# A gated delta-rule attention layer with experts on one core: bias and identity products leave TensorE, the inverse is merged by VectorE, and the order of the four engines' work is another

## The reference

```python
x = x + layernorm(attn(layernorm(x)))
x = x + layernorm(ffn(layernorm(x)))

# attn: 8 key heads, 16 value heads of 128
mixed = silu(causal_conv4(h @ Wqkv.T + bqkv) + conv_b)      # q, k, v
z     = h @ Wz.T + bz                                       # 2048 gate values
beta  = sigmoid(h @ Wb.T + bb)
g     = -exp(A_log) * softplus(h @ Wa.T + ba + dt_bias)
q = q * rsqrt(sum(q*q) + 1e-6) * 128**-0.5
k = k * rsqrt(sum(k*k) + 1e-6)
def step(state, (q, k, v, g, b)):                           # over the tokens
    state = state * exp(g)
    delta = (v - k @ state) * b
    state = state + outer(k, delta)
    return state, q @ state
core = outs * rsqrt(mean(outs*outs) + 1e-6) * norm_w * silu(z)
attn = core @ Wout.T + bout

# ffn: one shared expert, and the top 8 of 16 small ones
```

## Time and profile before

| | |
|---|---|
| median of 3 runs | 3621.46 us (3620.43 to 3624.41) |
| the profiled execution, its own time | 3620.91 us |
| its span in the trace | 3619.1 us |
| busy share of the span | PE 91%, VectorE 75%, ScalarE 67%, GpSimd 60% |
| first load issued, first matmul starts | 7.8 us, 68.3 us |
| one chunk of the loop | 108.0 us, of which TensorE is busy 101.5 us |
| the loads of the start, all behind one semaphore | 13.2 MB, landed by 44.5 us |
| granted TensorE clock | 0.966 of full over the span |

### The profile page before, as it was taken

How to read it: one execution, slowest core, us unless ns; L and a number is a source line. 1 busy time by engine, 2 the same in 40 slices (tenths; PEclk the granted TensorE clock), 3 DMA queues, 4 the chain that set the end, 5 groups by cost and what they waited for, 6 DMA issues and landing times.

```text
span 3619.1 us, 86991 instructions
## 1 busy us (share of the span) xinstructions
PE 3296.9 (91%) x24003; PEld 2944.1 (81%) x24256; DVE 2712.9 (75%) x8608; ACT 2441.7 (67%) x5922; POOL 2162.0 (60%) x5380
## 2 busy tenths in 40 slices
PE   1799999999999999999999999999999999999986
PEld 1688888888888888888888888888888888888875
DVE  3577787777787877777877778777777877777763
ACT  1576777767777667677677676676676667676662
POOL 0676666666666666666666666666566666566660
PEclk9899999999999999999999999999999999999996
DMA  3111111111111111111111111111111111111110
GB/s 156 37 43 34 41 35 35 41 38 33 41 34 35 43 35 34 43 32 41 38 35 41 36 32 42 36 35 40 36 32 40 38 35 40 37 32 42 36 40 4
DMA packets 423099, 142.70 MB, mean 39 GB/s; under 512 B 211120, under 2 KB 421616, under 8 KB 422128
## 3 DMA queue, kind: packets, MB, share of 16 engines
q1 hardware_dynamic: 422768, 139.83, 14.9%
HBM read 93.11 MB, written 46.66 MB: 39 GB/s over the span
## 4 chain that ended last, share of the span: by engine, by line
PE 66%; DVE 10%; ACT 10%; issue 9%; DMA 1%; POOL 1%; SPq 1%; DVEq 0%; ACTq 0%; POOLq 0%
PE bF L450 9%; PE bB L617 6%; PE bQ L530 5%; PE bXT L538 5%; PE bS L587 4%; PE bS L595 3%; PE bB L674 3%; ACT L793 3%; PE bB L668 3%; PE bS L579 2%; PE bD L602 2%; PE bQ L469 2%; PE bX L543 2%; PE bXT L477 2%; PE bD L580 2%
## 5 line engine op out<-in xcount | busy, mean ns | idle before, releaser
L1101 DVE SCALAR_TENSOR_TENSOR Y<-bF,Cv,Y 128x127 f32<-128x127 f32 (+2 forms) x3072 | 851.3, 338 | 18.0 <-ACT Y L810 13.2
L881 ACT ACTIVATE XiT<-bXT 128x512 fp32r<-128x512 f32 x384 | 229.5, 598 | 534.0 <-PE bXT L538 534.0
L450 PE MATMUL bF<-XnT,Wqkv 128*128 128x128 f32 x4096 | 549.0, 284 | 0.0
L450 PEld LDWEIGHTS bF<-XnT,Wqkv 128*128 128x128 f32 x4096 | 521.2, 200 | 7.0 <-issue 1.7
L810 ACT ACTIVATE Y<-bF,Cv 128x128 f32<-128x128 f32 x1024 | 385.2, 461 | 83.5 <-PE bF L450 83.5
L1517 POOL TENSOR_TENSOR Tp<-Tp 32x64 f32<-32x64 f32 (+2 forms) x768 | 359.8, 468 | 60.2
L1144 DVE TENSOR_TENSOR Qi<-bQ,Cf 128x512 fp32r<-128x512 f32 x384 | 265.0, 690 | 127.3 <-PE bQ L530 126.9
L793 ACT ACT_TABLE_LOAD x257 | 329.7, 1283 | 5.3 <-PEq L1601 0.7
L1510 POOL TENSOR_TENSOR Tp<-Cb,Yb 32x64 f32<-32x64 f32 (+1 forms) x384 | 275.5, 717 | 32.7 <-POOL Yb L1519 4.9
L1510 POOL TENSOR_TENSOR Tp<-Yb,Tm 32x64 f32<-32x64 f32 (+1 forms) x384 | 274.7, 715 | 30.1
L1411 POOL TENSOR_TENSOR Ln<-Ex,KKQ 128x512 f32<-128x512 f32 x128 | 164.2, 1283 | 207.5 <-ACT Ex L872 132.1
(11 more groups left out here) (217 smaller groups left out, 9335.2 us busy)
## 6 DMA issues: line engine op xcount, KB each, us to landing
DL<-Ln SPq DMA_DIRECT2D x128, 256.0 KB, 2.3
XiT<-DX SPq DMA_DIRECT2D x128, 256.0 KB, 2.9
Xi<-DX SPq DMA_DIRECT2D x128, 256.0 KB, 3.3
DX<-Yb SPq DMA_DIRECT2D x256, 32.0 KB, 1.9
Xf<-x SPq DMA_DIRECT2D x32, 128.0 KB, 2.8
Wqkv<-wqkv SPq DMA_DIRECT2D x1, 4096.0 KB, 15.8
Cb<-DL SPq DMA_DIRECT2D x128, 32.0 KB, 1.9
Xr<-x SPq DMA_DIRECT2D x32, 128.0 KB, 2.9
```

The lines of the kernel that those rows point to most:

```text
L450: last = mm(bank[:, i, :], Wqkv[:, k, c:c + P], XnT[:, k, :], start=(k == 0), stop=(k == KT - 1))
L881: op(XiT[:, :, :], heads(bXT), ACT.Copy).then_inc(sem["xt_done"], 1)
L1101: last = stt(y, bank[:, i, 0:P - shift], Cv[:, g * TILES + tile, n:n + 1], y, ALU.mult, ALU.add)
```

## The change

Six edits come together.

1. **Loads.** Five small transfers get a semaphore of their own (`early`), are issued first, and alone hold up the setup. `Wqkv` comes in four pieces; `Wz`, the z bias and the rest have semaphores that their first readers wait for. `Wout` is scaled by VectorE ahead of its first use.
2. **Biases.** No bias products: VectorE adds the z bias (kept as f32 in `Zf`) out of PSUM into `Gz` (`gate_bias`), and ScalarE takes the SiLU of `Gz` in place; the bias of beta and a is added where VectorE copied them before.
3. **Sums of squares.** `ss` is gone. TensorE transposes all four of q and k (two before), and ScalarE squares the transposed tiles in four instructions that also sum along the row (`accum_out`). The squares now follow the transposes.
4. **No identity products.** `invert_begin` is gone. VectorE adds level 0 out of PSUM to the `XiT` and `Xi` that the DMA brought (`merged_t`, `merged`), and ScalarE copies for levels 1 and 2 only the new off-diagonal blocks.
5. **The last level** works on 64 rows and 64 columns.
6. **Another order** of the steps on every engine. `proj(a, 1, 1)` moves ahead of `az`, `D0` from the head of item 2 to the end of item 1, `ba` from the end of item 0 to the head of item 1, `ks_qs(w, 1)` behind level 0.

```diff
             def z_proj(f, part):
                 if part == 0:
                     pe.wait_ge(sem["convv_done"], at("convv_done", f))
-                    mm(bF1[:, :], onesb, Zb[:, c], start=True, stop=False)
-                    mm(bF1[:, :], XnT[:, 0, :], Wz[:, 0, c], start=False, stop=False)
+                    mm(bF1[:, :], XnT[:, 0, :], Wz[:, 0, c], start=True, stop=False)
-            def ss(f):
...
-                for i in range(2 * GK):
-                    last = mm(bXT[:, i:i + 1], Sq[:, i, :], ones[:, 0:1], start=True, stop=True)
             def ktr(f):
-                pe.wait_ge(sem["sse_done"], at("sse_done", f))
-                for kh in range(GK):
-                    last = nc.tensor.transpose(heads(bXT)[:, kh, :], QK[:, g, 2 * kh + 1, :], ident)
+                pe.wait_ge(sem["xt_done"], at("xt_done", ahead(f, -2)))
+                pe.wait_ge(sem["silu_done"], at("silu_done", f, 1))
+                for i in range(2 * GK):
+                    last = nc.tensor.transpose(heads(bXT)[:, i, :], QK[:, g, i, :], ident)
-            def invert_begin(v, front):
...
-                mm(bXT[:, :], IdR[:, 0, :], XiT[:, :, :], start=True, stop=True)
-                mm(bX[:, :], IdR[:, 0, :], Xi[:, :, :], start=True, stop=True)
+            def invert_q(v, n, front=None):
                 if n == 0:
+                    if front:
+                        pe.wait_ge(sem["ex_done"], at("ex_done", ahead(v, 1)))
...
+                    pe.wait_ge(sem["xb_in"], at("xb_in", v))
                     pe.wait_ge(sem["lnr_done"], at("lnr_done", v))
...
             def square_qk(f):
-                op(Sq[:, :, :], QK[:, f[1], :, :], ACT.Square).then_inc(sem["sq_done"], 1)
+                act.wait_ge(sem["ktr_full"], at("ktr_full", f))
+                for i in range(2 * GK):
+                    last = op(Sq[:, i, :], heads(bXT)[:, i, :], ACT.Square, accum_out=Ssq[:, i:i + 1])
             def gate(f):
-                op(Gz[:, f[1], :, :], heads(bF1), ACT.Silu).then_inc(sem["gz_done"], 1)
+                act.wait_ge(sem["zb_done"], at("zb_done", f))
+                op(Gz[:, f[1], :, :], Gz[:, f[1], :, :], ACT.Silu).then_inc(sem["gz_done"], 1)
+            def new_blocks(bank, buf, n, below):
+                b = BASE << n
+                for o in range(0, P, 2 * b):
+                    rows, cols = slice(o + b, o + 2 * b), slice(o, o + b)
+                    if not below:
+                        rows, cols = cols, rows
+                    last = op(buf[rows, :, cols], heads(bank)[rows, :, cols], ACT.Copy)
+                return last
+            def gate_bias(f):
...
+                tt(Gz[:, g, :, :].rearrange("p a b -> p (a b)"), bF1[:, :], Zf[:, g * GH * P:(g + 1) * GH * P], ALU.add)\
+                    .then_inc(sem["zb_done"], 1)
+            def merged_t(v):
+                dve.wait_ge(sem["xt_full"], at("xt_full", v, 1))
+                tt(XiT[:, :, :], heads(bXT), XiT[:, :, :].bitcast(F32), ALU.add).then_inc(sem["xt_done"], 1)
+            def merged(v):
+                dve.wait_ge(sem["x_full"], at("x_full", v, 1))
+                tt(Xi[:, :, :], heads(bX), Xi[:, :, :].bitcast(F32), ALU.add).then_inc(sem["xi_done"], 1)
+        EARLY = [(whole(d), src) for d, src in ((Xf, x[0]), (Cf, constf), (Cv, conv), (Wba, wba))]
+        EARLY += [(Gz[:, :, :, :].rearrange("p a b c -> p (a b c)")[:, 0:14 * P], consth)]
```

353 lines of the change are left out of this document (186 added, 167 removed).

## The result

The changed kernel takes 3700.53 us (median of 4 runs, 3694.61 to 3703.16) against 3620.94 (3618.95 to 3624.41) in the same job: ratio 1.0216, 95% interval 1.0199 to 1.0234. The prediction was 3600 with a range of 3500 to 3670, so it was wrong by 100 us, in sign and beyond its range. The profiled run has 3702.07 us and a span of 3700.3.

The account below looks back on a forecast made before the run. TensorE was taken as the bound, with little of its saved work felt because of the chain at each item's head. From 3620.9 us, −46 for the start and +24 for the loop gave 3599, said as 3600; range 3500 to 3670.

Parts of the forecast that it names:

- The start: Setup before the loop: early loads end sooner, first matmul near 22 us, 46 us earlier (lower bound 35).
- The squares: Head of an item on ScalarE: four squares out of PSUM take 1.1 us, upper bound 1.4.
- Merges and gate's bias at 0.68 us each: VectorE: two merges and the gate's bias, 0.68 us each; +1.8 us an item with a third saved.
- The head, 10.6 us to the first inversion product: Item 2, start to the inverse's first product through ScalarE's chain to `Ex`: 10.6 us, before 10.5.
- my 28.0 and 25.5: Forecast lengths in us of item 1 (before 25.8) and item 2 (before 25.9).
- VectorE becomes the bound: Rival, chance 0.25: merges and gate's bias felt in full in item 1, chunk +3.0 us, time 3665.
- The wait for `Ex` that I gave as a sign: Ahead of the inverse's first product: TensorE waits 1 us or more for ScalarE's `Ex` in every item.
- The sum by item, +0.8 us a chunk: Loop: four items sum to 108.8 us against 108.0, +0.8 us a chunk, +24 us in 30 chunks.
- VectorE's pause at the loop's turn stays as it is: Loop's turn: VectorE's pause unchanged, its list still ending with the result's two steps; slower clock behind it stays too.
- TensorE's work, 1.41 us an item less: TensorE per item: sums of squares and identity products go, z bias halves, two transposes come; 5.6 us a chunk less.
- the signs: What would show it right: among others, TensorE busy 88 to 90%, about 96 of a chunk's 109 us.
- my sum: Whole kernel: 3620.9 − 46 + 24 = 3599 us, given as 3600.

Follow-up runs that it names:

- before_start_products: Kernel before with the new start alone, both biases still TensorE products, the z bias split on 128x16: 3590.6 us, 0.9926 of before.
- changed_identity: Changed kernel with the first level's identity products and ScalarE's two full copies back in place of VectorE's merges: 3736.4 us, 1.0332 of before.
- changed_bias_product: Changed kernel with both biases as TensorE products again, 238 satisfied waits keeping TensorE's loop in its place: 3727.0 us, 1.0310 of before.
- order_fits: Changed kernel with bias and first-level identity products of before, Epq on ScalarE, waits ahead of all four lists against turn pauses: 3629.4 us, 1.0037 of before.
- start_fits_turn: start_and_turn with the small product Epq moved from VectorE to ScalarE, so VectorE's loop lies in three blocks: 3446.0 us, 0.9530 of before.
- turn_changed_60: Changed kernel with 60 more instructions (satisfied waits) ahead of TensorE's list, the loop itself the same: 3765.2 us, 1.0411 of before.
- start_and_turn: before_start_products with VectorE's list 23 and GpSimd's 20 instructions longer ahead of the loop: 3585.5 us, 0.9911 of before.
- changed_again: The changed kernel itself once more, unaltered, as reference for the runs beside it: 3692.8 us, 1.0220 of before.
- before_vector_fits: Kernel before with 21 more instructions (satisfied waits) ahead of VectorE's list: 3615.4 us, 0.9996 of before.

## Why the prediction was wrong, step by step

- *The start*: first matmul at 22.52 us, forecast 22, 45.8 us earlier. VectorE's chain begins at 17.07. Right. That the kernel would gain all of it was not: before_start_products gained 26 us.
- *The squares*: four in 1.00 us from start to start (1822.58 to 1823.58), forecast 1.1; 0.9 by the formula of the Trainium skill, "ScalarE: Activation LUTs". Between the two. The changed kernel's rows show what the formula leaves out, a second record each:

```profile
1822.58 0.30 ACT L843 ACTIVATE Sq<-bXT 128x128 f32<-128x128 f32 x1
1822.74 0.23 ACT L843 ACTIVATION_READ_ACCUMULATOR Sq<-bXT 128x1 f32 x1
1822.83 0.31 ACT L843 ACTIVATE Sq<-bXT 128x128 f32<-128x128 f32 x1
```

- *Merges and gate's bias at 0.68 us each*: 0.685, 0.679 and 0.690. Right. Taking them away gained nothing (changed_identity, changed_bias_product): the rival "VectorE becomes the bound" is refuted as a mechanism, though its time, 3665, was nearer. That was luck.
- *The head, 10.6 us to the first inversion product*: 11.09 in item 2 (1817.93 to 1829.02). `PartsT` began at 8.95, where I had it finished at 8.94; its 0.32 us and the hand-over make TensorE wait 0.66. That 0.5 us is as much as items 1 and 2 each have over my 28.0 and 25.5; that it is the same 0.5 us is not shown. The wait for `Ex` that I gave as a sign, 1 us or more in every item, is 0.43 us in three items of four; the chain is felt at three places instead, at Z, `PartsT` and `Ex`.

```profile
1826.88 0.32 ACT L875 ACTIVATE PartsT<-bXT 128x128 bf16<-128x128 bf16 x1
1827.55 0.38 PE L515 MATMUL bQ<-PartsT,Ch 128*128 128x128 bf16 x4 [0.66 <-ACT PartsT L875]
1829.02 0.63 PE L538 MATMUL bQ<-XiT,LnR 128*128 128x128 f32 x4 [0.43 <-ACT Ex L888]
```

- *The sum by item, +0.8 us a chunk*: this is the step that failed; the loop has +3.8. It took the order as nearly free. Where nothing pauses (order_fits against start_fits_turn), items 0 to 3 take 1.4, 2.6, 0.5 and 1.4 us more, with the bias and identity products still in. I had −1.1, +2.2, −0.4 and +0.1: the terms that were mis-sized are those of items 0 and 3 above all, where the head should have got shorter or stayed.
- *"VectorE's pause at the loop's turn stays as it is"*: its 2.7 us did stay. But I had nothing for pauses of TensorE's own, which came with the place of its shorter loop: 84 us in 29 turns, 2.9 a chunk. The first of them, 1.7 us, ends item 3, which has 29.6 us where I had 27.1; turn_changed_60, without it, has 27.7. So item 3 is over by 1.8 for the pause and 0.6 besides, items 1 and 2 by 0.5 each, and item 0 is under by 0.8 (27.4 for 28.2): 2.6 of the 2.7 us that the medians leave open. These 1.8 us are where the pause stands and not its price: turn_changed_60 took it away and got slower.
- *TensorE's work, 1.41 us an item less*: the signs had 96 us of a chunk busy, and it is 100. The sums of squares and the identity products went at about their price (3.4 and 2.2 us a chunk by start to next start). But groups that now stand ahead of a wait last longer: `new_state` 4.7 us a chunk instead of 3.6, `out_proj` 7.5 instead of 6.4. A cost read from start to next start in a full list leaves out the end of the last product, which a wait uncovers; that this is the reason is argued, not tested.
- *Whether the turn is to blame for the loss*: the pairs of runs do not say so. The turn costs the old order 4.8 us a chunk (start_and_turn against start_fits_turn). Against order_fits it costs the changed kernel 2.6 us (111.8 against 109.2). The bias and identity products are in order_fits and not in the changed kernel; changed_bias_product and changed_identity have 0.5 and 1.0 us a chunk more than changed_again, which gives 4.1 us for the turn as an estimate, and 4.3 of the 5.8 for the order. So the order with its head made the loop slower; the pauses changed places, and no run shows that they became dearer.
- *The first chunks*: I had nothing for them, and they cost 20 us. Without the change's order they cost 2 (before_start_products: 96.4 and 104.3 us against 94.6 and 103.9); order_fits has 101.4 and 110.4. The rest of chunk 0, 108.8, is not settled; its granted clock is 0.92 where before had 0.98, and the same kernel in changed_again has 104.2.
- *The sum*: 29 chunks at +3.8 instead of +0.8 make 86 of the 103 us between the profiled time and my sum; the first two 19; the start came 2 short and the tail gave 4.
- *What I did not see at all*: that the 108.0 us of before held 4.6 us of pause and slower clock a chunk (103.4 without). My forecast kept it as a constant on both sides; it was worth three times what the new start saves.

Shown: the pauses and their dependence on place (for TensorE, GpSimd and VectorE), the taps, the 5.8 us of order, squares and copies together. Argued only: the split of that 5.8 us beyond the taps (by the trace the head's waits for Z, `PartsT` and `Ex` are 2.4, 1.5 and 1.3 us a chunk), and the clock's part in turn_changed_60. The changed operations in the old order were not tried as a whole, nor the changed kernel with a VectorE loop that fits: its 407 instructions are too many for three blocks.

## What to carry to other kernels

Look at the branch and at the queues that fetch instructions before any order of work: if they move packets in steady state, an engine stops at every turn, and a few instructions less, or some more ahead of the loop, can be worth more than a rewrite (here 138 us for four instructions less in a loop and some 50 more ahead of it). Changing a tuned loop's length or start moves this for every engine, so compare versions only with it under control. And a dependent chain at the head of a pipelined item costs at each of its hand-overs, even where the bounding engine's sum of work falls.

## What the runs showed of the hardware that I had not expected

- TensorE's loop ran without fetching while it touched seven blocks of 256 instructions, and fetched nine blocks a turn when it touched eight, the last of them by 39 instructions (q8: 279 packets); with 14 it did so in one turn of 30 (28 packets). VectorE's and GpSimd's did without up to three blocks of 128; four instructions in a fourth cost VectorE 2.7 us each turn (before_vector_fits). ScalarE (loops of 288 and 308 instructions) never paused at the turn; where its borders lie, no run shows.
- A turn that misses has two pauses: one at the branch, one where the first block ends (medians: TensorE 1.8 and 1.2 us; VectorE 2.7 to 2.8 and 0.5 to 2.4; GpSimd 2.1 and 1.8). The second is no constant: at the same instruction VectorE stood for 0.6 us in the changed kernel and for 1.6 in turn_changed_60.
- One wait of 4.8 us ahead of `core_t` was followed by products at half the granted clock in the turn shown. With TensorE's two pauses and nine products between them (medians 1.8 and 1.2 us), the clock fell in the first 7 us of item 0 in 3 of 29 turns; with four products between (1.4 and 1.9 us) in 24 of 29.
